# Local-attention stack on one core: masks seeded by VectorE, one gated block of the FFN moved, turned chunks ahead of the projection

## The reference

```python
for i in range(6):                       # DEPTH
    x = attn_layer(shift_tokens(x), ...) + x
    x = ffn_layer(shift_tokens(x), ...) + x

def attn_layer(x, Wqkv, qs, ksc, Wo):
    q, k, v = split(x @ Wqkv)            # 3 x 1024 columns, float32
    q = l2norm(q) * qs; k = l2norm(k) * ksc
    q = q*cos*scale + rotate_half(q)*sin*scale       # and k, by 1/scale
    sim = where(mask, -max, windows(q) @ windows(k) * 8)
    return softmax(sim) @ windows(v) @ Wo

def ffn_layer(x, ...):
    a, gate = split(layernorm(x) * g + b @ W1 + b1)  # 341 columns each
    return a * gelu(gate) @ W2 + b2
```

## Time and profile before

| | |
|---|---|
| median of 3 runs | 2707.03 us |
| profiled execution, its own time | 2708.14 us |
| its span, first to last instruction | 2706.4 us |
| TensorE clock granted, mean | 0.964 |
| TensorE busy | 2462.3 us (91%) |
| VectorE, ScalarE, GpSimd busy | 1677.8, 1581.8, 1607.0 us (58 to 62%) |

### The profile page before, as it was taken

How to read it: one execution, slowest core, us unless ns; L and a number is a source line. 1 busy time by engine, 2 the same in 40 slices (tenths; PEclk the granted TensorE clock), 3 DMA queues, 4 the chain that set the end, 5 groups by cost and what they waited for, 6 DMA issues and landing times.

```text
span 2706.4 us, 57956 instructions
## 1 busy us (share of the span) xinstructions
PE 2462.3 (91%) x23054; PEld 1687.6 (62%) x23054; DVE 1677.8 (62%) x2517; ACT 1581.8 (58%) x3162; POOL 1607.0 (59%) x931
## 2 busy tenths in 40 slices
PE   5769999999999999999999999999997888889998
PEld 3435666666666666666666666666664666656665
DVE  2347667666766666666666666766672888852222
ACT  1126666666666676667666666666662566643333
POOL 1039777777777777777777777777771322211111
PEclk8769999999999999999999999999997899989999
DMA  4002223222232222322233222322223000000000
GB/s 103 0 20 60 53 52 72 64 62 50 57 75 64 55 53 61 74 65 53 53 74 72 52 52 52 80 64 55 50 55 104 1 1 1 1 1 1 5 5 8
DMA packets 77196, 127.13 MB, mean 47 GB/s; under 512 B 24948, under 2 KB 48770, under 8 KB 76930
## 3 DMA queue, kind: packets, MB, share of 16 engines
q1 hardware_dynamic: 76930, 123.42, 19.6%
HBM read 26.56 MB, written 1.07 MB: 10 GB/s over the span
## 4 chain that ended last, share of the span: by engine, by line
PE 49%; DVE 20%; ACT 16%; issue 12%; POOL 3%; SPq 0%; DMA 0%; POOLq 0%; ACTq 0%; DVEq 0%
PE bank L601 6%; PE bank L526 6%; DVE qk L1200 6%; ACT qk L891 5%; PE bank L804 4%; PE bank L613 4%; PE bank L563 4%; PE obank L583 3%; ACT vp L903 3%; PE obank L814 2%; PE bank L814 2%; DVE n L1207 2%; PE bank L738 2%; PE lnbank L547 2%; ACT aoT L936 2%
## 5 line engine op out<-in xcount | busy, mean ns | idle before, releaser
L1200 DVE TENSOR_TENSOR qk<-bank,tab 128x1024 f32<-128x1024 f32 x384 | 470.3, 1225 | 438.2 <-ACT qk L891 438.2
L1497 POOL TENSOR_TENSOR qk<-qk 128x1024 f32<-128x1024 f32 x192 | 454.0, 2365 | 362.3 <-DVE qk L1200 362.2
L1501 POOL TENSOR_TENSOR rn<-n2m,cst 128x16 f32<-128x16 f32 x192 | 562.9, 2932 | 16.0
L526 PE MATMUL bank<-wqk,xs 128*128 128x512 f32 x768 | 400.5, 603 | 6.2 <-issue 3.7
L1505 POOL TENSOR_TENSOR qk<-qk,rn 128x1024 f32<-128x1024 f32 x192 | 365.4, 1903 | 28.1 <-POOL rn L1501 0.9
L891 ACT ACTIVATE qk<-bank 128x512 f32<-128x512 f32 x384 | 228.7, 596 | 173.2 <-PE bank L526 165.2
L537 PEld LDWEIGHTS bank<-cst,qk 128*128 128x128 f32 x1536 | 192.4, 141 | 209.8 <-issue 197.4
L1509 POOL TENSOR_TENSOR lnr<-lnv,cst 128x2 f32<-128x2 f32 (+1 forms) x88 | 66.4, 755 | 404.1 <-DVE lnv L1094 404.1
L924 ACT ACTIVATE px<-sh 128x512 f32<-128x512 f32 x192 | 121.4, 632 | 256.2 <-DVE sh L1216 255.6
L537 PE MATMUL bank<-cst,qk 128*128 128x128 f32 x1536 | 231.7, 274 | 6.6 <-POOL qk L1505 6.6
L1207 DVE TENSOR_REDUCE n<-qk 128x16 f32<-128x1024 f32 x192 | 232.2, 1209 | 0.0
(11 more groups left out here) (194 smaller groups left out, 4429.1 us busy)
## 6 DMA issues: line engine op xcount, KB each, us to landing
vp<-vp SPq DMA_DIRECT2D x672, 130.0 KB, 2.4
wqk<-in_L_ffn_Wqkv SPq DMA_DIRECT2D x24, 256.0 KB, 3.1
wv<-in_L_ffn_Wqkv SPq DMA_DIRECT2D x6, 512.0 KB, 3.6
wo<-in_L_ffn_Wo SPq DMA_DIRECT2D x6, 512.0 KB, 4.3
xs<-Z SPq DMA_DIRECT2D x48, 64.0 KB, 2.4
xs<-Z SPq DMA_DIRECT2D x48, 63.8 KB, 2.3
kT<-rel_by_distance SPq DMA_DIRECT2D x1, 2048.0 KB, 7.9
vp<-in_L_ffn_w SPq DMA_DIRECT2D x1, 2048.0 KB, 13.3
```

The costliest lines, as they stand in the source:

```text
L526: nc.tensor.matmul(bank[s % 2][:, :], xs[:, odd, WIN + r * P:WIN + r * P + P], wqk[:, lo:lo + 512], start=True, stop=True).then_inc(p_full, 1)
L1200: tt(qk[:, both, :].rearrange("p o (h d) -> p o h d", d=DH), heads(bank[c % 2][:, :]).unsqueeze(1).broadcast_to([P, 2, PAIRS, DH]), table. ...
L1497: tt(direct, direct, swapped, ALU.add).then_inc(sum_done, 1)
L1501: tt(rn[:, m % 2, :], n2m[:, :], const("mhalf"), ALU.pow).then_inc(rn_done, 1)
```

## The change

1. `scores` has no mask matmul. VectorE copies the mask (bf16 in SBUF) into `bank[3]` (`seed`), after the subtraction of the last scores; the bank's written bits are set once by a matmul at the start. `scores` waits for `seeded` instead of `pt_done`.
2. `turn_probs` writes into the first bank of `obank`, and `take_probs` reads it there.
3. FFN block 1 goes through `bank[4]` and from slot 5 into slot 6, behind the projection; its gelu and gate follow. Block 2 waits for the gate of block 0 alone, block 1 for `take_out`, and `turn_out` in slot 7 for the gate of block 1.
4. `turn` stands ahead of `projection` in each slot; on ScalarE `take_turned` ahead of `squares`.
5. `ln_wide_pe` uses transpositions instead of float32 matmuls, in every stage.
6. ScalarE's `take_values` comes one slot later; its layer-norm square stands at the head of slot 2, and VectorE's `ln_d_dve` ahead of `parts` in slot 2.

```diff
 def ln_wide_pe(w, u, b=lnbank):
-  mm = nc.tensor.matmul(b[:, i * P:i * P + P], lnr[:, i:i + 1].broadcast_to([P, P]), ident,
-                        start=True, stop=True)
+  mm = nc.tensor.transpose(b[:, i * P:i * P + P], lnr[:, i:i + 1].broadcast_to([P, P]), ident)
 def scores(i, k):
-  wait(pe, pt_done, 4 * i + k)
+  pe.wait_ge(seeded, 4 * i + k + 1)
-  nc.tensor.matmul(s[:, :], ident_bf, maskv[:, r, :], start=True, stop=False, skip_group_check=True)
 def turn_probs(i, k):
   pe.wait_ge(px_done, 4 * i + k + 1)
+  wait(pe, ao_done, 4 * i + k)
-    mm = nc.tensor.transpose(bank[3][:, q * P:q * P + P], ...)
+    mm = nc.tensor.transpose(obank[:, 0, :][:, q * P:q * P + P], ...)
 def turn_out(i, k):
+  if k == 3 and i >= 1:
+    pe.wait_ge(h_done, 3 * i - 1)
 def hidden(i, c):
-  else:
-    pe.wait_ge(h_done, 3 * i + c)
+  if c == 1:
+    wait(pe, ot_done, 4 * i + 4 + min(3, 4 * (ITEMS - 1 - i)))
+  if c == 2:
+    pe.wait_ge(h_done, 3 * i + 1)
 # TensorE, in each slot
-  if p0:
-    projection(t, s, odd)
   if s >= LAG and p0:
     turn(t, s - LAG, s)
   if s < LAG and p1:
     turn(i, s + 8 - LAG, s, not p0)
+  if p0:
+    projection(t, s, odd)
+  if s == 6 and p2:
+    hidden(f, 1)
...
-  if s in (4, 5, 6) and p2:
+  if s in (4, 6) and p2:
     hidden(f, s - 4)
 # ScalarE, in each slot
-  if s in (5, 6, 7) and p2:
+  if s in (5, 7) and p2:
     gelu(f, s - 5)
-  if p0:
-    squares(t, s)
+  if s == 2 and p2:
+    ln_sq_act(S, LN_S2 + f)
   if s >= LAG and p0:
     take_turned(t, s - LAG, s)
   if s < LAG and p1:
     take_turned(i, s + 8 - LAG, s)
+  if p0:
+    squares(t, s)
+  if s == 6 and p2:
+    gelu(f, 1)
-  if s in (3, 5, 7) and p0:
-    take_values(t, s // 2 - 1)
-  if s == 1 and p1:
-    take_values(i, 3)
+  if s in (4, 6) and p0:
+    take_values(t, s // 2 - 2)
+  if s in (0, 2) and p1:
+    take_values(i, s // 2 + 2)
 # VectorE
+def seed(i, k):
+  n = 4 * i + k + 1
+  if n < 4 * ITEMS:
+    dve.wait_ge(sh_done, n)
+    nc.vector.tensor_copy(bank[3][:, :], maskv[:, (n % 4) // 2, :]).then_inc(seeded, 1)
+  if s == 2 and p2:                      # now ahead of parts
+    ln_d_dve(xf[:, :], S, LN_S2 + f, bank[2])
+  if s == 7 and p2:
+    gate(f, 2)
   if p0:
     parts(t, s)
+  if s in (5, 6) and p2:                 # behind parts
+    gate(f, s - 5)
...
+  if s in (1, 3, 5) and p1:              # behind norms
+    seed(i, s // 2 + 1)
+  if s == 7 and p0:
+    seed(t, 0)
```

More of the change, by code:

```diff
@@ L70 @@
 LAG = 4
+HD_BANK = (2, 4, 2)
 GATE_OPS, TAIL_OPS = 13, 6
@@ L245, in build @@
         mx_done, sh_done, px_done = sem("mx_done"), sem("sh_done"), sem("px_done")
+        seeded = sem("seeded")
         pt_full, pt_done = sem("pt_full"), sem("pt_done")
@@ L569, in turn_probs @@
                 pe.wait_ge(px_done, 4 * i + k + 1)
+                wait(pe, ao_done, 4 * i + k)
                 for q in range(4):
-                    mm = nc.tensor.transpose(bank[3][:, q * P:q * P + P], px[:, k % 2, q * P:q * P + P], ident)
+                    mm = nc.tensor.transpose(obank[:, 0, :][:, q * P:q * P + P], px[:, k % 2, q * P:q * P + P], ident)
                 mm.then_inc(pt_full, 1)
@@ L608, in hidden @@
                     pe.wait_ge(ld_w1, (i // B) * 16 + 16)
-                else:
-                    pe.wait_ge(h_done, 3 * i + c)
+                if c == 1:
+                    wait(pe, ot_done, 4 * i + 4 + min(3, 4 * (ITEMS - 1 - i)))
+                if c == 2:
+                    pe.wait_ge(h_done, 3 * i + 1)
                 n = P if c < 2 else FFR
                 for half in range(2):
-                    mm = nc.tensor.matmul(bank[2][0:n, half * S:half * S + S], w1[:, half * FF + c * P:half * FF + c * P + n],
+                    mm = nc.tensor.matmul(bank[HD_BANK[c]][0:n, half * S:half * S + S], w1[:, half * FF + c * P:half * FF + c * P + n],
                                           lnt[:, S:2 * S], start=True, stop=True)
@@ L663, in _ @@
             pe.wait_ge(masks_cast, 1)
+            nc.tensor.matmul(bank[3][:, :], ident_bf, maskv[:, 0, :], start=True, stop=True).then_inc(seeded, 1)
             step(0, 0, True, False, False, False)
@@ L928, in take_probs @@
                 wait(act, o_full, 4 * i + k - 1)
-                nc.scalar.copy(pT[:, k % 2, :], bank[3][:, :]).then_inc(pt_done, 1)
+                nc.scalar.copy(pT[:, k % 2, :], obank[:, 0, :]).then_inc(pt_done, 1)
             def take_out(i, k):
@@ L941, in gelu @@
                 act.wait_ge(hd_full, 3 * i + c + 1)
-                nc.scalar.activation(ge[0:n, c, :], bank[2][0:n, S:2 * S], ACT.Gelu,
+                nc.scalar.activation(ge[0:n, c, :], bank[HD_BANK[c]][0:n, S:2 * S], ACT.Gelu,
                                      bias=b1g[0:n, c, bass.ds(i // B, 1)]).then_inc(ge_done, 1)
@@ L963, in step @@
                         nc.scalar.copy(xf[64:P, 1:S], Z[64:P, f % B, 0:S - 1]).then_inc(xf_ready, 1)
-                    if s == 2 and p2:
-                        ln_sq_act(S, LN_S2 + f)
-                    if s in (3, 5, 7) and p0:
-                        take_values(t, s // 2 - 1)
-                    if s == 1 and p1:
-                        take_values(i, 3)
+                    if s in (4, 6) and p0:
+                        take_values(t, s // 2 - 2)
+                    if s in (0, 2) and p1:
+                        take_values(i, s // 2 + 2)
                     if s % 2 == 1 and p1:
@@ L1245, in gate @@
                 dve.wait_ge(ge_done, 3 * i + c + 1)
-                nc.vector.scalar_tensor_tensor(out=hT[0:n, c, :], in0=bank[2][0:n, 0:S], scalar=b1a[0:n, c, l],
+                nc.vector.scalar_tensor_tensor(out=hT[0:n, c, :], in0=bank[HD_BANK[c]][0:n, 0:S], scalar=b1a[0:n, c, l],
                                                in1=ge[0:n, c, :], op0=ALU.add, op1=ALU.mult).then_inc(h_done, 1)
@@ L1265, in step @@
                         scale_norm(f)
-                    if s in (6, 7) and p2:
-                        gate(f, s - 5)
+                    if s == 2 and p2:
+                        ln_d_dve(xf[:, :], S, LN_S2 + f, bank[2])
+                    if s == 7 and p2:
+                        gate(f, 2)
                     if p0:
                         parts(t, s)
[L1270 to L1273, removed]
+                    if s in (5, 6) and p2:
+                        gate(f, s - 5)
                     if s in (0, 2, 4) and p1:
```

## The result

The changed kernel takes 2874.9 us (median of four runs) against 2706.6: a ratio of 1.0617 (95% interval 1.0599 to 1.0636), 168 us slower. The forecast was 2818, slower by 4.1%. That is 111 us of the 168.

What follows compares the result with a forecast made beforehand. TensorE was taken to bound the kernel before; after the change, a 41.5 us loop across engines against 38.96. 2708.1 + 117 (46 steps x 2.5) - 6 (transpositions) = 2819.1, as median 2818 us; range 2713 to 2905.

Steps and rivals of the forecast that it cites:

- The step that decided: Turn ahead of projection, copies ahead of squares: the loop takes 41.5 us a step against 38.96, 2.5 us more.
- legs: Loop between turns of slots 0, 1, 6, FFN block 2 and next slot 0: 7.20, 23.6, 4.17, 6.50 us.
- leg 2: Turn of slot 1 to turn of slot 6, all on ScalarE and VectorE: 23.6 us.
- four times 1.07: On ScalarE, k's two copies ahead of the squares: about 1.07 us for each of four pairs.
- The summed case: Loop over all engines as added up: 41.5 us a step, 2818 us, spanning 2780 to 2865; chance 0.66.
- the rival of held seeds: VectorE's seeds wait for GpSimd's addition: 2.5 us a step more, 44.0 us, about 2933 us; chance 0.07.
- the 6 us of the transpositions: Wide layer-norm transpositions outside the stack, half of their instructions gone: between 0 and 22 us less, 6 taken.
- the looser loop: Some links shorter than their rows, or seed at 0.42: 39.1 to 40.7 us a step, 2713 to 2780; chance 0.12.
- Savings: TensorE: mask matmuls 1.24, block 1's wait 1.09, bank waits 0.80, layer-norm transpositions 0.22; 38.96 - 3.35 = 35.6 us a step.
- the relay: ScalarE, VectorE and TensorE handing over in list order; as a loop it takes 41.5 us a step.
- The seed at 0.69 and not 0.42: VectorE's mask copy into PSUM takes 0.69 us at single rate; the fast rate would shorten the step about 0.5 us.
- The rival that TensorE stays the bound: Loop shorter than TensorE's 35.6 us a step, so all 3.35 us are saved: 2548 us; chance 0.09.

Runs made afterwards that it cites:

- the fastest version: Changed kernel with both engines' order undone, block 0's gelu and table load behind ScalarE's copies, slot 7's seed ahead of norms: 2536.8 us, 0.9376 of the kernel before.

## Why the prediction was right, and where it was short

- **The step that decided, that the turn's place and the copies' place make a loop of ScalarE and VectorE longer than TensorE's work**, is shown: undoing it alone turns 1.062 into 0.963, and doing it alone gives 1.067. Its size: 41.5 us forecast, 41.93 measured in undisturbed steps, legs of 7.18, 23.94, 5.81 (with 1.63 by the clock, so 4.18) and 6.63. 0.43 x 46 = 20 us short; most of it, 0.3, is in leg 2. Within the loop the copies weigh most (235 of 269 us, or 254 when the projection is first), near what was summed (four times 1.07), and not the turn being asked for early (33 or 15). The same walk was less exact on other orders, 0.3 to 1.1 us a step short. The prediction also had TensorE waiting for turns in all of slots 2 to 6; the trace has such waits in 3, 4 and 6, and that of slot 3 is 0.5 us, not 1.
- **What was short is the clock.** The text named an idle stretch of about 2.5 us in slot 6 (measured 2.36) and that a fall of the clock would make things worse, but gave it neither a price nor a chance. It came in 25 of 46 steps at 1.63 us each: 41 us. Together, 2819 + 20 + 41 = 2880, less about 6 by which the time outside the 46 full steps came out better than counted, is about the 2875 measured.
- **That the time fell into the range is in part luck.** The summed case was given 2780 to 2865, and 2875 is above that. The range reached to 2905 for the rival of held seeds, which did not come, and not for the clock. Besides, 2865 doesn't follow from the terms beside it: half a microsecond on 46 steps and the 6 us of the transpositions on top of 2818 give 2847. Nor does 39.1 us a step, the lower end of the looser loop, give 2713: by the same sum it gives 2707.
- **Outside the full steps** two errors cancelled. The partial steps were put at nothing, but the first output projection starts at 239.1 us in the changed kernel and at 230.2 with the order undone: the order costs 9 us there too. The wide products alone bring 9 us in the same place (229.7 for 238.6). The 12 us by which the rest is shorter lie in the last distance (3) and behind the last output projection (9); the wide products explain 1 of them, and the others stay open.
- **Savings**: the mask matmuls, the wait of block 1 and the wait for the bank are gone from TensorE. Together they are worth about what they were said to be once the relay is out of the way: 3.19 us a step in the fastest version (38.95 to 35.76), of the 3.35 counted. Of the single terms only the wide products were tested, and they brought 16 us as counted, but by the trace 3 to 4 in the steps and the rest outside them, instead of 10 and 6.
- **The seed at 0.69 and not 0.42** was right (0.68). The Trainium skill, VectorE: DVE Perf Modes, Why PSUM operands drop a tier, says that a float32 operand in PSUM keeps VectorE at its single rate. The trace agrees: the seed is as long as the subtraction of 512 elements out of PSUM (0.69). That a seed of slot 3 is free because the scale is held by GpSimd anyway was right (3.75 for 3.77). The rival of seeds held up by GpSimd did not come: all 191 seeds took 0.68 to 0.69 us, those beside GpSimd too. Nor did the looser loop: the step was above the sum and not below it.
- **The rival that TensorE stays the bound**, at 2548 us, is what the change comes to once its order is undone and the table load stands last (2548.9). That these two agree to a microsecond is chance: the experiment's steps are 35.97 us where the rival has 35.6, and more came off outside them.
- The other engines (GpSimd, the v copies and DMAs a slot later) cost nothing; no turn of the steady steps waits for GpSimd.

## What to carry to other kernels

Ahead of swapping two steps in hand-ordered engine lists, walk the loop over all engines once, with start-to-start distances from the timeline: what stands behind a wait in one list delays all that follows in it, and engines that are idle for over a third of the time can still form the longest loop. In such a list an operation that releases another engine (here the squares) belongs ahead of one that has slack (the copies) and a table load behind both. Watch not only the consumer that was moved, but everything that waits for the operations now last in line. And give a price to a clock that may fall in an idle stretch, once the walk shows such a stretch.

## What the hardware showed that was not expected

- A recurring idle stretch of TensorE of 2.36 us, once a step, was followed by the lower clock in 25 of 46 steps, for over 3 us, at 1.63 us a time. So it was in 24 of 46 with 2.75 us (the order alone) and in 13 of 46 with 2.45 us (the masks by TensorE). With 1.04 us of idle time in the same place it never was, nor in the steps of any other version, where TensorE's longest wait in a step is 1.17 us or less.
- Adding twelve useless transpositions a step to that place made the kernel 46 us faster.
- A VectorE cast from bf16 in SBUF to float32 in PSUM, 128x512, takes 0.68 us, also with a GpSimd operation on SBUF beside it.
